# A two-layer transformer on one core: the first attention's division, GpSimd's instructions and the expert gathers rewritten

## The reference

```python
x = x + 0.5 * L0_ffn(ln(x))      # 8 experts, hidden 256, top 2 of sigmoid scores, relu squared; all experts computed
x = x + L0_attn(ln(x))           # 32 heads of 32; softmax(q k / sqrt(32)) v; w_out, then a layer norm
x = x + 0.5 * L0_ffn(ln(x))
x = x + 0.5 * L1_ffn(ln(x))      # 8 experts, hidden 512, top 2, capacity 640 tokens each: gathered, silu(g)*u, scattered
x = x + L1_attn(ln(x))           # 16 heads of 64; softmax(q k / 8) v; w_out
x = x + 0.5 * L1_ffn(ln(x))
```

## Time and profile before

| | us |
|---|---|
| median of 3 runs | 2975.75 (2974.71 to 2978.07) |
| the profiled execution | 2968.92 |
| its span, first to last instruction | 2967.0 |

### The profile page before, as it was taken

One profiled execution on the slowest core, in us unless ns is written; L12 is line 12 of the kernel. 1 busy time (PEld: TensorE's weight loads), 2 busy tenths in 40 slices (PEclk: granted clock), 3 DMA queues, 4 the chain that ended last, 5 costly groups with the idle time before them and its releaser, 6 DMA issues. The chain is left out here.

```text
span 2967.0 us, 53680 instructions
## 1 busy us (share of the span) xinstructions
PE 2662.9 (90%) x19444; PEld 1854.4 (63%) x19444; DVE 1997.3 (67%) x4630; ACT 1941.4 (65%) x4045; POOL 2063.0 (70%) x1668
## 2 busy tenths in 40 slices
PE   7999999999999999998997486999999999998376
PEld 6996565656565665656886385565565665665276
DVE  5667777777777777775776643767677677676632
ACT  5665767777767777676775144878778778777133
POOL 0003989898989889894110285989889889889067
PEclk9999999999999999999998697999999999999588
DMA  3014545444544454440001143000000000000033
GB/s 103 1 58 117 124 109 124 113 117 113 127 108 118 112 122 108 114 102 15 19 16 47 60 85 51 1 2 9 8 2 9 9 2 9 8 2 9 29 84 53
DMA packets 144661, 179.34 MB, mean 60 GB/s; under 512 B 30547, under 2 KB 74128, under 8 KB 143888
## 3 DMA queue, kind: packets, MB, share of 16 engines
q1 hardware_dynamic: 130320, 165.20, 22.0%
q0 software_dynamic: 14080, 10.73, 2.7%
HBM read 56.51 MB, written 17.72 MB: 25 GB/s over the span
## 5 line engine op out<-in xcount | busy, mean ns | idle before, releaser
L2062 POOL TENSOR_TENSOR arena<-arena 128x512 f32<-128x512 f32 x768 | 963.7, 1287 | 187.9 <-ACT arena L1364 172.7
L1673 DVE TENSOR_REDUCE top<-psum 128x1 f32<-128x512 f32 x1024 | 643.5, 677 | 72.9 <-PE psum L932 72.4
L932 PE MATMUL psum<-stack 96*128 96x512 f32 (+1 forms) x2048 | 628.6, 427 | 16.7 <-ACT arena L1364 9.6
L1364 ACT ACTIVATE arena<-psum 128x512 f32<-128x512 f32 x1024 | 564.2, 602 | 100.5 <-PE psum L932 98.2
L2074 POOL TENSOR_SCALAR by_query<-by_query,row_tables 128x512 f32<-128x512 f32 x340 | 527.3, 1569 | 44.7 <-DVE row_tables L1679 43.3
L1003 PE MATMUL psum<-arena,values 128*32 128x512 f32 (+1 forms) x3072 | 482.4, 600 | 4.4 <-ACT arena L1364 3.4
L932 PEld LDWEIGHTS psum<-stack 96*128 96x128 f32 (+1 forms) x2048 | 345.6, 191 | 197.9 <-DVE top L1673 85.7
L1671 DVE TENSOR_REDUCE row_tables<-psum 128x1 f32<-128x512 f32 x512 | 339.9, 682 | 45.8 <-PE psum L940 44.9
L1003 PEld LDWEIGHTS psum<-arena,values 128*32 128x32 f32 (+1 forms) x3072 | 128.7, 119 | 278.7 <-issue 269.3
L2074 POOL TENSOR_SCALAR arena<-arena,row_tables 128x512 f32<-128x512 f32 x172 | 267.4, 1571 | 46.1 <-DVE row_tables L1679 45.4
L2031 POOL TENSOR_SCALAR rstd<-mv 128x4 f32<-128x4 f32 x56 | 13.2, 236 | 409.6 <-DVE mv L1537 407.1
(11 more groups left out here) (202 smaller groups left out, 4718.6 us busy)
## 6 DMA issues: line engine op xcount, KB each, us to landing
stack<-halves SPq DMA_DIRECT2D x768, 128.0 KB, 2.3
qk_ring<-qk_split SPq DMA_DIRECT2D x64, 256.0 KB, 2.9
v_ring<-v_split SPq DMA_DIRECT2D x32, 256.0 KB, 3.0
tokens<-xn SPq DMA_DIRECT2D x16, 256.0 KB, 2.4
arena<-in_wg SPq DMA_DIRECT2D x16, 256.0 KB, 3.0
arena<-in_wu SPq DMA_DIRECT2D x16, 256.0 KB, 3.4
arena<-in_wd SPq DMA_DIRECT2D x16, 256.0 KB, 3.0
wqkv<-in_w_qkv SPq DMA_DIRECT2D x2, 1536.0 KB, 9.3
```

The costliest lines, as they stand in the source:

```text
L932: return T_.matmul(bk, st[0:k, side, h, cols], st[0:k, 1 - side, h, :], start=True, stop=True)
L1364: S_.activation(prob[tile % N_PROB][:, h, :], psum[:, bank[key], :], ACT.Exp, scale=scale).then_inc(released[bank[key]], 1)
L1673: give(V_.reduce_max(top[i][:, j:j + 1], psum[:, bank[key], :], AX.X), key)
L2062: ins = G_.tensor_tensor(to[:, h, :], old[:, h, :], prob[tile % N_PROB][:, h, :], ALU.add)
```

## The change

Five edits, and new positions.

1. `mix` of the first attention: ACT takes the natural logarithm of the sums from PSUM and then exp(-that), in place; DVE refines this near inverse r with the sums d, first d*r, then (d*r - 2)*r, and multiplies the weighted values by its negative. The eight transpositions, the reciprocal and the spreading are gone. A table set with both functions is loaded for groups 0, 62 and 63.
2. The addition of `prob` tiles is one POOL instruction of 128x2048.
3. The scaling of a query tile is one POOL instruction, a product of 128x1024 by the two shares, broadcast.
4. `rows_in` has 8 places, six of them in an idle stack buffer. POOL issues the gathers of 20 tiles first, then 4 before the scatters of each expert from 1 on. The last product of an expert is split into 2 and 3 tiles instead of 4 and 1.
5. `mixed[1]` has 10 places.

```diff
-    dict(project=(-0.110, 0.700), maxima=(0.980, 1.840), rows=(1.950, 1.950), probs=(2.250, 3.170),
-         last=(3.250, 3.370), mix=(3.940, 4.550), out=(4.530, 5.010), ahead=(-2.310, -0.790),
+    dict(project=(-0.221, 0.718), maxima=(1.027, 1.942), rows=(1.950, 1.950), probs=(2.294, 3.170),
+         last=(3.292, 3.292), mix=(3.940, 3.954), out=(4.445, 4.761), ahead=(-2.284, -0.764),
...
-    dict(queries=(0.615, 0.660), keys=(0.605, 0.605), values=(1.177, 1.210), maxima=(1.000, 1.750),
-         exps=(1.048, 1.808), shares=(1.340, 2.257), turns=(1.896, 2.647), last=(2.753, 2.877), out=(3.443, 3.443),
+    dict(queries=(0.677, 0.722), keys=(0.674, 0.674), values=(1.205, 1.205),
+         maxima=[1.000, 1.094, 1.188, 1.358, 1.452, 1.469, 1.562, 1.656],
+         exps=[1.085, 1.186, 1.286, 1.387, 1.488, 1.589, 1.690, 1.790], shares=[1.340, 1.569, 1.799, 2.028],
...
+AHEAD, BETWEEN = 4, 4
+NARROW = ((0, 2), (2, SLOT_TILES))
...
             def mix(l, n):            # ACT
-                r = inverse[n % 2]
-                key = ("dn", l, n)
+                near, key = inverse[n % 2], ("dn", l, n)
                 if n >= 2:
-                    act.wait_ge(*written(("back", l, n - 2)))
+                    act.wait_ge(*divided(l, n - 2))
                 act.wait_ge(*written(key))
-                S_.activation(r, psum[:, bank[key], :], ACT.Copy).then_inc(released[bank[key]], 1)
-                yield
-                yield
-                act.wait_ge(*written(("turned", l, n)))
-                act.wait_ge(*read(("turned", l, n)))
-                S_.activation(r.rearrange("p (t h w) -> p t h w", t=TILES_B, h=HEADS[l]),
-                              recips[n % 2][:, :, :].unsqueeze(3).to_broadcast([P, TILES_B, HEADS[l], WIDTH[l]]),
-                              ACT.Copy).then_inc(spread, 1)
+                if n == 0 or n + 2 >= N_GROUPS:
+                    S_.preload_act_table_set("natural_log_exp_and_others")
+                S_.activation(near, psum[:, bank[key], :], ACT.Ln).then_inc(logged, 1)
+                act.wait_ge(logged, n + 1)
+                S_.activation(near, near, ACT.Exp, scale=-1.0).then_inc(inverse_near, 1)
                 yield
...
             def mix(l, n):            # DVE
+                dn = psum[:, bank[key], :]
+                yield
+                dve.wait_ge(inverse_near, n + 1)
+                done = tick(V_.tensor_tensor(dn, dn, inverse[i], ALU.mult))
+                yield
+                dve.wait_ge(*done)
+                done = tick(V_.scalar_tensor_tensor(out=dn, in0=dn, scalar=2.0, in1=inverse[i],
+                                                    op0=ALU.subtract, op1=ALU.mult))
                 yield
...
-                dve.wait_ge(*written(back))
-                give(V_.tensor_tensor(mixed[l][:, g, :], weighted[i], psum[:, bank[back], :], ALU.mult), back)
+                dve.wait_ge(*done)
+                give(V_.scalar_tensor_tensor(out=mixed[l][:, g, :], in0=weighted[i], scalar=-1.0, in1=dn,
+                                             op0=ALU.mult, op1=ALU.mult), key)
...
-                        for h in range(heads):
-                            ins = G_.tensor_tensor(to[:, h, :], old[:, h, :], prob[tile % N_PROB][:, h, :], ALU.add)
-                        ins.then_inc(summed, 1)
+                        G_.tensor_tensor(to, old, prob[tile % N_PROB], ALU.add).then_inc(summed, 1)
...
-                    for h in range(HEADS[1]):
-                        rows = by_query[(at * HEADS[1] + h) % N_ROWS]
-                        G_.tensor_scalar(rows, rows, row_share[n % 2][:, qt, h:h + 1], None, ALU.mult).then_inc(scaled, 1)
+                    rows = by_query[at % len(by_query)]
+                    G_.tensor_tensor(rows[:, :, :], rows[:, :, :], row_share[n % 2][:, qt, :].unsqueeze(2).to_broadcast(
+                        [P, HEADS[1], SEQ]), ALU.mult).then_inc(scaled, 1)
...
-                gather_rows(0)
-                gather_rows(1)
+                gathered = AHEAD * SLOT_TILES
+                gather_rows(range(gathered))
                 for e in range(EXPERTS):
-                    if e + 2 < EXPERTS:
-                        gather_rows(e + 2)
+                    if e:
+                        more = min(gathered + BETWEEN, SLOT_ROWS)
+                        gather_rows(range(gathered, more))
+                        gathered = more
                     scatter_rows(e)
```

More of the change, by code:

```diff
@@ L94, in flush, with spread @@
         streams.clear()
+    def spread(where, calls, steps):
+        if isinstance(where, list):
+            return where
+        start, end = where
+        return [start + (end - start) * i / steps for i in range(calls)]
     def experts0(s, at, routed):
@@ L119, in queue @@
         def queue(part, numbers, calls, steps, n):
-            start, end = WHEN[l][part]
+            where = spread(WHEN[l][part], calls, steps)
             part = dict(ranks="route", queries="project", keys="project", values="project").get(part, part)
-            stream(part, numbers, calls, steps, at + n + start, at + n + end)
+            for here in where:
+                stream(part, numbers, 1, 1, at + n + here, at + n + here)
         for n in range(N_GROUPS):
@@ L135, in attention @@
                 queue("probs", (l, n), heads * TILES_B + 1, heads * TILES_B + 1, n)
-                start, end = WHEN[l]["probs"]
-                pair = start + (end - start) * 3 * heads / (heads * TILES_B + 1)
+                pair = spread(WHEN[l]["probs"], heads * TILES_B + 1, heads * TILES_B + 1)[3 * heads]
                 stream("sums", (l, n), 1, 1, at + n + 1 + pair - 0.001, at + n + 1 + pair - 0.001)
-                queue("mix", (l, n), 5, 5, n)
+                queue("mix", (l, n), 4, 4, n)
             else:
@@ L339, in mix @@
     def mix(self, l, n):
-        dn, turned, back = ("dn", l, n), ("turned", l, n), ("back", l, n)
-        if l == 0:
-            self.other.give(dn)
+        for _ in range(TILES_B if l else 3):
             yield
-            self.other.take(turned)
-            yield
-            self.other.give(turned)
-            yield
[L348 to L356, removed]
+        self.other.give(("dn", l, n))
+        yield
     def out(self, l, b):
@@ L774, in divided @@
         def divided(l, n):
-            return read(("o", 1, n)) if l else read(("back", l, n))
+            return read(("o", 1, n)) if l else read(("dn", l, n))
         def last_of_slot(n_slots, slot):
@@ L1040, in sums_of @@
                 yield
[L1042 to L1052, removed]
-                bk, done = place(("back", l, n))
-                turn(bk, columns).then_inc(done, 1)
-                yield
             def project_out(l, b):
@@ L1175, in _ @@
             play(order, dict(prepare0=prepare0, route=route, ahead=ahead, compute0=compute0, project=project,
-                             maxima=maxima, rows=rows_of_maxima, probs=probabilities, turns=turns, last=last_tiles, sums=sums_of, mix=mix,
+                             maxima=maxima, rows=rows_of_maxima, probs=probabilities, turns=turns, last=last_tiles, sums=sums_of,
                              out=project_out, fold=fold, experts1=experts1))
@@ L1401, in last_tiles @@
                     yield
-                if l and g:
-                    pass
+                if l and n >= N_MIXED:
+                    act.wait_ge(*written(("out", 1, (n - N_MIXED) // GROUPS)))
                 elif l:
-                    act.wait_ge(*(written(("out", 1, b - 1)) if b else arena_free(1)))
+                    act.wait_ge(*arena_free(1))
                 elif n >= 2:
@@ L1496, in experts1 @@
                     act.wait_ge(slot_weights, s * EXPERTS + e + 1)
-                    for part, (lo, hi) in enumerate(((0, 4), (4, SLOT_TILES))):
+                    for part, (lo, hi) in enumerate(NARROW):
                         key = ("narrow", s, e, part)
@@ L2081, in experts1, with gather_rows @@
             def experts1(s):
[L2082 to L2083 removed]
+                def gather_rows(numbers):
                     pool.wait_ge(*read(("tokens", s)))
```

78 lines of the change are left out of this document (37 added, 41 removed).

## The result

| | us, median (lowest to highest) | ratio to the kernel before, 95% interval |
|---|---|---|
| before | 2976.91 (2974.71 to 2978.22, 4 runs) | |
| changed | 2880.28 (2877.77 to 2883.45, 4 runs) | 0.9677 [0.9662, 0.9691] |

The change saves 96.6 us; the forecast was 101. The profiled execution of the changed kernel has a span of 2877.2 us, 89.8 less than before, at the same mean granted clock (0.952 and 0.953).

A forecast was written before the change was run, and what follows sets the result against it. PE, POOL close behind, paces the first attention; POOL between `out` blocks and PE in them the second; POOL the experts. -40 - 49 - 14 + 2 = -101 from 2968.9 gives 2867.9, the median 6.8 above: 2875 us; range 2823 to 2935.

The forecast's parts named there:

- Division without turning: First attention: dropping eight PE transpositions a group, together with the merged addition, saves 0.62 us a group, 40 us.
- One addition: First attention: one POOL addition of 128x2048 takes 4.57 us against 5.15; its saving is counted within the division's 40 us.
- One scaling: Second attention: one POOL scaling takes 2.38 us, not 3.09, and POOL stops bounding; 6.1 us a batch, 49 us.
- Gathers ahead: Expert loops: 20 gathers first, then 4 instead of 5 for experts 1 to 5; 7 us a loop, 14 us.
- Ten places, the split: Second attention's mixed[1] places and the experts' last product: worth 0, the places at most 1 us either way.
- Positions: Both attentions: new positions only cover the division's new DVE passes; counted as nothing else, -10 to +10.
- Rival A: Both attentions: another wait, for DVE or ACT, takes POOL's place, saving 23 and 20 us; 2921 us, chance 0.22.
- B: Both attentions: PE reaches its floor, 103.6 us a batch in the second; saves 153 us, 2823 us, chance 0.17.
- C: Second attention: the product with a broadcast operand is dear, 4.6 us a tile; slower, 3308 us, chance 0.05.
- D: Both attentions: parts cancel, scaling near 3.2 us a tile and DVE late in the first; within 0.2%, chance 0.02.
- the fixed price that I read from the rows: Second attention: a DVE instruction with two SBUF inputs takes 0.24 us more beside POOL scalings; 2 us a batch, hidden.
- the exclusion for a whole instruction: Second attention: by the skill's rule some 8 DVE routing steps a batch each wait up to 2.4 us for POOL; 10 us.

The follow-up runs named there:

- e5: The changed kernel again, unaltered; 2862.79 us, ratio to before 0.9651.
- e6: The changed kernel with all positions of the kernel before, all other edits kept; 2925.12 us, ratio to before 0.9852.
- e7: The changed kernel with the old division by turning, in five calls from 3.940 to 4.550, other positions new; 2931.68 us, ratio to before 0.9877.
- e3: The changed kernel with eight idle transpositions of the identity on PE ahead of each group's sums; 2917.18 us, ratio to before 0.9831.
- e2: The changed kernel with each addition of prob tiles as four instructions of 128x512 again; 2866.73 us, ratio to before 0.9666.
- e12: The changed kernel with 15 gathers ahead and 5 between, run beside an unaltered control; 2877.39 us, ratio to before 0.9693.
- e11: The changed kernel a fourth time, unaltered, as control for 15 gathers ahead on the same chip; 2862.70 us, ratio to before 0.9644.
- e8: The changed kernel with eight places in mixed[1] and the last product split 4/1 again; 2866.04 us, ratio to before 0.9653.
- e10: The changed kernel with old positions and two scalings a query tile together; 2956.62 us, ratio to before 0.9948.
- e1: The changed kernel with a query tile's scaling as two instructions of 128x512 again; 2897.89 us, ratio to before 0.9767.
- e9: The changed kernel a third time, unaltered, on another chip; 2883.08 us, ratio to before 0.9699.
- e4: The changed kernel with 15 gathers ahead and 5 between, as before, but all eight places; 2876.90 us, ratio to before 0.9692.

## Why the prediction was right, step by step

The time and the direction held; the ledger by stage held for the two attentions together, and for the expert loops only where nothing stalls. From the traces of before, changed and e5 (us saved):

| stretch | forecast | changed | e5 |
|---|---|---|---|
| start to first gather | 38 | 47.9 | 49.3 |
| first gather to last scatter, first loop | 7 | -0.8 | 8.5 |
| to the first full `out`, and from it to the last | 49 | 10.5 + 36.2 | 11.4 + 36.1 |
| from there to the last scatter | 7 | -1.9 | 7.4 |
| end | 0 | -2.0 | -2.0 |
| sum | 101 | 89.8 | 110.7 |

That the first profile came so close is partly luck, because two errors cancel: the first attention gave 10 us more, and the stalls took 19. Luck, too, is that 49 for the second attention came in: it was put down to the single scaling, which alone gives 10 (point 6).

1. *Division without turning, 0.62 us a group.* The mechanism is right, and so is the price of a transposition. I added up PE's time from each matmul's start to the next in the traces, us a batch, mean of the four from the second `out` block to the sixth:

   | | batch | the 256 score products | transpositions of the sums |
   |---|---|---|---|
   | before | 138.2 | 70.6 | 5.7 |
   | e6, new division, old positions | 136.6 | 74.2 | 0 |
   | e7, old division, new positions | 141.9 | 74.8 | 5.7 |
   | e5, both new | 131.8 | 70.0 | 0 |
   | e3, e5 with eight idle ones | 138.2 | 68.8 | 7.7 |

   Eight transpositions cost 0.71 us a group (forecast 0.70), 46 us of the 49 that the stretch gained; my sum had taken 40 and 2 off for the tables. e3's idle ones, eight in a row, cost 0.97 and overstate it. But the gain comes only with positions that fit: with old ones the score products take 3.6 us a batch more than before and eat most of it. Neighbouring sums stand 16.3 us apart before, 16.0 in e6, 16.6 in e7 and 15.3 in e5 (medians; forecast 16.1). Also, "134.5 us a batch, 16.8 a group" was misread: from one `out` block to the next it is 1101.73 - 963.89 = 137.8 us before and 1193.17 - 1061.85 = 131.3 in e5. The sum did not rest on it. DVE's new passes (0.70, 0.70, 0.69) were covered for the most part, at 84% busy from 300 to 1300 us. A table load takes 1283 ns, and the ACTIVATE behind it starts 1.29 us after it does, so the drain that the prediction quotes does not show here; there are four more loads than before (24 against 20), 5 us of ACT.
2. *One addition.* Its price was right (4.57 forecast, 4.59 measured), its use was not: e2 loses nothing. POOL's waits for ACT's exponentials (200.3 us over the kernel, 125.0 in e2) are slack, of which four short additions used a part.
3. *One scaling.* Mis-sized price, right saving for the stage, but not by this edit alone (point 6). 1.90 us instead of 2.38 frees 15 us more of POOL a batch, but nothing comes of it, since PE no longer waits for POOL. The bottom of my range assumed that a read of a repeated operand costs as much as that of a fresh one. The batch fell 5.5 us, inside the 2.9 to 9.2 I had allowed, and 107 to 108 us was forecast. The stage as a whole saved 47 us against 49.
4. *Gathers ahead.* Right within 2 us where nothing stalls: 8.5 and 7.4 us against 7 and 7. Of these the order of the gathers is 5.8 and 5.7 (e12 against e11). In the first profile both loops stall for some 9.4 us, and nothing is left of it.
5. *Ten places, the split.* Nothing in the times (e8). By e8's one trace the split may bring 1 to 3 us a loop, which is what the gathers' order leaves of the 8.5 and 7.4; other traces differ by nearly as much among themselves, so this is not shown.
6. *Positions, "as the cover of part 1 and as nothing else; -10 to +10".* This step failed. They are worth 62 us with the other edits in place, about half of it in the second attention. As cover they were not needed: with the old positions DVE never waits for the exponential from 300 to 1300 us, with the new ones it waits 36.7. What they change is that PE's score products come 4.2 us a batch faster (74.2 to 70.0), while DVE's wait for ACT's copy (65.1 us in 600 before), which I had counted as cover only, goes; that the one is the cause of the other is likely but not shown. And I had not followed the second attention's new list of positions at all. The total held all the same, because I had priced the other edits as if their positions fitted: e6 and e7 show that with the wrong ones most of the gain is not there.

In the first attention four cells show it, the start of the first gather (before adds in four instructions, the others in one, which e2 puts at 4 us or less):

| | old division | new division |
|---|---|---|
| old positions | 1678.4 (before) | 1661.5 (e6) |
| new positions | 1699.2 (e7) | 1629.1 (e5) |

The new positions lose 21 us with the old division and gain 32 with the new one. The second attention has four such cells, us between the first and the last full `out`:

| | two scalings | one scaling |
|---|---|---|
| old positions | 787.0 (e10) | 777.5 (e6) |
| new positions | 778.3 (e1) | 751.3 (e5) |

Alone each gives 9 to 10; together 36. With two scalings POOL holds PE whatever the order. With old positions PE stays slow once POOL is out of the way, and the rows that remain are the hand-offs between PE, ACT and DVE (e6); that these hold it is argued, not tested. Rival A had this mechanism: another wait does take POOL's place, unless the order of work is changed with it. B's floor of 103.6 us a batch is 4.6 us away. C and D are refuted by the 1898 ns.

Open: what the stalls are. They occurred in both loops, while POOL issues its gathers, from about the 13th on, in the changed kernel's first trace, in e9 and in e10; not in e1 to e8, e11, e12 or before. Each chip of e1 to e12 showed them either in all traces or in none, 9.4 us a loop, 19 in all, and the changed kernel's medians follow: 2880 (first) and 2883 (e9) with stalls, 2863 both times on e5's chip without. 20 gathers ahead are not enough to bring them. The kernel before, with 15, took 2971.4 us on e9's chip and 2967.0 to 2968.9 on those without stalls, so it hardly has them there; but it differs in other things too, and e4's kernel did not come to such a chip. In the first runs it took 2976.9, 8 to 10 us more than on the chips without stalls, and its one trace, an execution of 2968.9, need not be from that chip; so whether it stalls there is open as well. Which of the new positions makes the 26 us in the second attention was not tried either.

## What to carry to other kernels

Removing a bound and reordering the work behind it are one change: test the four cells before crediting either, since here each alone gave 9 or 10 us of 36 in one stage, and in the other the new order alone lost 21. An idle stand-in for a removed instruction shows whether its engine is the bound, but its price need not be that of the original (0.12 us against 0.09 here): compare start-to-start distances in both traces. When an engine's list is nearly full, count it: 40 gathers at 1.30 us and 40 scatters at 1.86 are 126 of the 132 us from the first gather's start to the last scatter's end, so no further order of gathers can shorten the loop by more than 6.

## What the runs showed of the hardware

A POOL product of 128x1024 with an operand that repeats over 512 elements takes 1898 ns, so 1.66 ns an element over the 201 ns of a small one; with two full operands it is 2.14 to 2.15 (1287 ns at 512 elements, 4594 at 2048), and as a product by a scalar of each partition 1564 ns at 512 (e1), 2.68 over the same 201. The Trainium skill, "GPSIMD Engine Reference", section "Elementwise — side-by-side cycle accounting", gives two-input operations 2.6 cycles an element and puts it down to the read port. The addition agrees (4497 ns stated for 2048, 4594 here); the repeated operand is cheaper than that rule. It is also a product and not an addition, and no run separates the two.

One DVE line with two SBUF inputs took 426 ns in every batch beside 1.55 us scalings, and 424 in e10. In e5 it takes 172, but once 682 (line, ns min/median/max).

```profile
L1827 DVE SCALAR_TENSOR_TENSOR r_value<-arena,r_score x7: 171/172/682, 1984.0 to 2631.3; 128x32 f32<-128x32 f32 x7
```

Meeting a POOL instruction is not enough to slow it. In the kernel before it starts 0.30 us behind the start of a scaling, six times; in e1 it starts 0.71 to 1.06 us behind the start of one, seven times, with POOL as busy as before, and takes 169 to 174 ns (POOL's times in a trace are rough). So neither the fixed price that I read from the rows nor the exclusion for a whole instruction that the prediction quotes fits these traces; what decides is open.

The same program differs by 20 us between chips, at granted clocks that differ by 0.006 (0.952 and 0.958), almost all of it through the stalls in the expert loops; the spread of one chip's runs (2877.77 to 2883.45) does not show it.
